# Count units placed inside the tiles of O and the neighbour projections, and every fourth unit's source one-hots made by VectorE

## The reference

```
xn = layernorm(x)
x  = x + sage_2_layers(xn, src, dst) + linear_attention(xn)      # Wq Wk Wv Wo
x  = x + moe(layernorm(x))                                       # 8 experts, top 2, and a shared expert
sage layer: h @ W_self + (segment_sum(h[src], dst) / degree) @ W_neigh + b
attention:  q = softmax over 64 of xn Wq; k = softmax over the nodes; (q (k^T v)) Wo + bo
```

## Time and profile before

| what | value |
|---|---|
| median of three runs | 1117.62 us |
| the profiled execution's own time | 1117.01 us |
| its span, first to last instruction | 1115.2 us |
| TensorE busy over the span | 1095.0 us |
| stage of the change, from the first matmul of O(0,0) to the first of the next stage | 224.86 to 362.81 us |
| TensorE, VectorE, ScalarE busy in these 137.95 us | 128.59, 84.93, 110.62 us |
| TensorE busy in the 197 us after it (363 to 560) | 197.00 us |

### The profile page before, as it was taken

How to read it: one execution, slowest core, us unless ns; L and a number is a source line. 1 busy time by engine, 2 the same in 40 slices (tenths; PEclk the granted TensorE clock), 3 DMA queues, 4 the chain that set the end, 5 groups by cost and what they waited for, 6 DMA issues and landing times.

```text
span 1115.2 us, 16441 instructions
## 1 busy us (share of the span) xinstructions
PE 1095.0 (98%) x6225; PEld 948.3 (85%) x6225; DVE 638.7 (57%) x880; ACT 482.3 (43%) x712; POOL 66.0 (6%) x88
## 2 busy tenths in 40 slices
PE   7999999999999999999999999999999999999998
PEld 5889998877777999878789999888988988988876
DVE  6789955765566744343373522445646556556545
ACT  4503321477888312211234222235655646556550
POOL 2000000000000000000000430200000000000003
PEclk9999999999999999999999999999999999999999
DMA  7222211232322022722004442377486676666647
GB/s 249 76 76 77 76 39 38 76 104 76 104 76 76 1 76 76 261 76 76 1 1 169 153 110 76 118 265 273 170 291 224 218 262 225 237 226 220 237 168 280
DMA packets 76488, 157.01 MB, mean 141 GB/s; under 512 B 7160, under 2 KB 7432, under 8 KB 76432
## 3 DMA queue, kind: packets, MB, share of 16 engines
q1 hardware_dynamic: 64908, 127.30, 33.3%
q10 hardware_dynamic: 7300, 15.41, 3.8%
q0 software_dynamic: 4224, 13.55, 3.7%
HBM read 135.69 MB, written 20.54 MB: 140 GB/s over the span
## 4 chain that ended last, share of the span: by engine, by line
PE 86%; DVE 4%; DVEq 3%; DMA 2%; issue 2%; ACT 1%; POOL 1%; POOLq 0%; SPq 0%; ACTq 0%
PE ps L1643 21%; PE ps L1645 20%; PE ps L1644 20%; PE ps L2055 10%; PE ps L2056 5%; DVEq L1356 2%; PE ps L1682 1%; PE ps L1728 1%; PE ps L1958 1%; PE ps L1959 1%; PE ps L1889 1%; PE ps L1890 1%; DVE c_f L1348 1%; DVEq L1349 1%; DMA y_second<-expert_rows,slots 1%
## 5 line engine op out<-in xcount | busy, mean ns | idle before, releaser
L991 DVE TENSOR_TENSOR w_lo<-w_raw,w_hi 128x2048 fp32r<-128x2048 f32 x108 | 244.7, 2290 | 136.8 <-ACT w_hi L685 134.7
L685 ACT CAST w_hi<-w_raw 128x2048 fp32r<-128x2048 f32 x108 | 203.5, 1911 | 87.8 <-PE ps L1959 36.2
L2055 PE MATMUL ps<-xe,w_hi 128*128 128x448 f32 x512 | 160.9, 375 | 0.0
L2056 PE MATMUL ps<-xe,w_lo 128*128 128x224 f32 x512 | 134.8, 263 | 0.0
L2055 PEld LDWEIGHTS ps<-xe,w_hi 128*128 128x128 f32 x512 | 95.9, 187 | 7.9
L1643 PE MATMUL ps<-w_hi,xt_hi 128*128 128x512 f32 (+1 forms) x240 | 96.0, 400 | 5.5 <-DVEq L999 4.3
L1643 PE MATMUL ps<-w_hi,he_hi 128*128 128x512 f32 (+1 forms) x256 | 101.2, 395 | 0.0
L1645 PE MATMUL ps<-w_hi,he_lo 128*128 128x512 f32 (+1 forms) x256 | 100.2, 391 | 0.0
L1644 PE MATMUL ps<-w_lo,he_hi 128*128 128x512 f32 (+1 forms) x256 | 100.0, 391 | 0.0
L2056 PEld LDWEIGHTS ps<-xe,w_lo 128*128 128x128 f32 x512 | 97.5, 190 | 0.4
L1645 PE MATMUL ps<-w_hi,xt_lo 128*128 128x512 f32 (+1 forms) x240 | 93.7, 390 | 0.0
(11 more groups left out here) (324 smaller groups left out, 1984.1 us busy)
## 6 DMA issues: line engine op xcount, KB each, us to landing
w_raw<-in_L_ffn_w SPq DMA_DIRECT2D x64, 1024.0 KB
w_raw<-in_L_gnn_W_neigh SPq DMA_DIRECT2D x8, 1024.0 KB
w_raw<-in_L_gnn_W_self SPq DMA_DIRECT2D x8, 1024.0 KB
w_raw<-in_L_ffn_shared_gate_up SPq DMA_DIRECT2D x8, 1024.0 KB
w_raw<-in_L_mix_Wv SPq DMA_DIRECT2D x4, 1024.0 KB
w_raw<-in_L_mix_Wk SPq DMA_DIRECT2D x4, 1024.0 KB
w_raw<-in_L_mix_Wq SPq DMA_DIRECT2D x4, 1024.0 KB
w_raw<-in_L_mix_Wo SPq DMA_DIRECT2D x4, 1024.0 KB
```

What stands on the lines that cost most here:

```text
L685: copy(w_hi[b][:, s * HK:(s + 1) * HK, :], w_raw[s][:, :, :]).then_inc(hi_done, 1)
L991: V_.tensor_tensor(w_lo[b][:, k, :], w_raw[s][:, :, :], as32(w_hi[b][:, k, :]), ALU.subtract).then_inc(lo_done, 1)
L2055: mat(PS(key)[:, a, 0:2 * B], wh[:, k, w_cols], xe[:, :, k, 0:B], start=k == 0, stop=False)
L2056: last = mat(PS(key)[:, a, 0:B], wl[:, k, w_cols], xe_hi[:, k, 0:B], start=False, stop=k == KF - 1)
```

## The change

Three things are changed.

1. **Place of the units on TensorE.** The units of a tile are issued inside the tile, after its k-steps 2, 4 and 6 (counted from 0; `AFTER_K`), and no longer behind its last matmul. So 9 matmuls of the tile stand ahead of the first unit, 6 between two units and 3 behind a third.
2. **Order on VectorE and ScalarE.** Both now deal with the tile's units first (additions and one-hots), then take the tile itself out of PSUM, then make the quarter of weights.
3. **Source one-hots.** For u = 3, 7, 11, ... 47 (12 units) VectorE makes the source one-hots in one comparison of 128x512, in an order with the two chunks of a pair interleaved; TensorE then reads that unit's weights with a stride of two elements. A copy `src16` of the list is made once for it.

The hand-out changes by one unit: units 0 to 2 now belong to O(0,0), unit 3 to O(0,1). The numbers of units in the five tiles of the halves are O(0,.) 3, 1, 2, 3, 3 (before: 2, 2, 2, 3, 3), O(1,.) 3, 1, 2, 3, 3, G(0,.) 3, 2, 1, 3, 3 and G(1,.) 3, 2, 2, 3, 3.

```diff
-    weights_to = [sum(2 if key[2] in SPLIT_AT else 3.5 for key in mains[:m + 1]) for m in range(len(mains))]
+    weights_to = [sum(1.625 if key[2] in SPLIT_AT else 3 for key in mains[:m + 1]) for m in range(len(mains))]
...
+    AFTER_K = (2, 4, 6)
+    by_vector = lambda u: u % 4 == 3
+    of_scalar = lambda u: sum(not by_vector(g) for g in range(u + 1))
...
             def source_one_hots(g):
                 b = g % GBUF
+                if by_vector(g):
+                    return
...
             for key in mains:                                   # ScalarE
+                for u in counts_in[key]:
+                    if u + GBUF < CU and not by_vector(u + GBUF):
+                        wait_unit(("cnt", u))
+                        source_one_hots(u + GBUF)
                 (attention_store if key[0] == "o" else neighbour_hi)(*key[1:])
                 if key[2] in SPLIT_AT:
                     split_hi(next_job(key), quarters=(SPLIT_AT[key[2]],))
-                for u in counts_behind[key]:
-                    if u + GBUF < CU:
-                        wait_unit(("cnt", u))
-                        source_one_hots(u + GBUF)
...
+                V_.tensor_copy(src16[:, :], list_s[:, :])
...
+                if by_vector(g):
+                    pairs_128 = [128, PER, 128, IL]
+                    V_.tensor_tensor(src_pairs(b), iota_c[:, 0:128, :].unsqueeze(1).to_broadcast(pairs_128),
+                                     src16[:, of_group].rearrange("p (q c) -> p q c", c=IL).unsqueeze(2).to_broadcast(pairs_128),
+                                     ALU.is_equal)
...
             for key in mains:                                   # VectorE
-                bins_at = load_bins(counts_behind[key])
-                (attention_out if key[0] == "o" else neighbour_lo)(*key[1:])
-                for n, u in enumerate(counts_behind[key]):
+                bins_at = load_bins(counts_in[key])
+                for n, u in enumerate(counts_in[key]):
                     add_counts(u, bins_at[PER * n:PER * n + PER])
                     if u + GBUF < CU:
                         one_hots(u + GBUF)
+                (attention_out if key[0] == "o" else neighbour_lo)(*key[1:])
                 if key[2] in SPLIT_AT:
                     split_lo(next_job(key), quarters=(SPLIT_AT[key[2]],))
...
                     last = passes(out_ap, [t[:, k, tokens] for t in operand], (wh[:, k, :], wl[:, k, :]),
                                   start and k == 0, stop and k == KF - 1)
+                    for after, u in zip(AFTER_K, inside):
+                        if k == after:
+                            count(u)
...
-            for key in mixed:
-                if key[0] == "cnt":
-                    count(key[1])
-                elif key[0] == "o":
+            for key in mains:
+                if key[0] == "o":
```

More of the change, by code:

```diff
@@ L124, in gps_layer @@
     units += mixed
-    counts_behind = {key: [k[1] for k in mixed[n + 1:mixed.index(mains[m + 1]) if m + 1 < len(mains) else None]]
+    counts_in = {key: [k[1] for k in mixed[n + 1:mixed.index(mains[m + 1]) if m + 1 < len(mains) else None]]
                      for m, key in enumerate(mains) for n in [mixed.index(key)]}
+    assert max(len(us) for us in counts_in.values()) < RING
+    AFTER_K = (2, 4, 6)
+    by_vector = lambda u: u % 4 == 3
+    of_scalar = lambda u: sum(not by_vector(g) for g in range(u + 1))
     chunks_of = lambda u: range(u * PC, min((u + 1) * PC, NC))
@@ L320, in gps_layer @@
         dst16 = following("dst16", [128, LC], f16, 2)
+        src16 = following("src16", [128, LC], b16, 2)
         assert off[0] <= RC + RCS
@@ L417, in gps_layer @@
         by_half = lambda ap: ap.rearrange("p (c n) -> p c n", c=2)
+        src_pairs = lambda b: src_oh[b][:, :, :].rearrange("p g n -> p (g n)").rearrange("p (q n c) -> p q n c", q=PER, c=IL)
         def halved(t, k, p=128):
@@ L802, in source_one_hots @@
                                          bias=src_f[:, g * GC + c:g * GC + c + 1]).then_inc(src_abs, 1)
-                act.wait_ge(src_abs, (g + 1) * GC)
+                act.wait_ge(src_abs, of_scalar(g) * GC)
                 nc.scalar.activation(src_oh[b][:, :, :], src_oh[b][:, :, :], ACT.Relu, bias=1.0, scale=-1.0).then_inc(src_ready, 1)
@@ L1650, in weights, with by_tokens @@
                 return w_hi[job % 2], w_lo[job % 2]
-            def by_tokens(key, out_ap, operand, job, tokens, start=True, stop=True, arrives=None):
+            def by_tokens(key, out_ap, operand, job, tokens, start=True, stop=True, arrives=None, inside=()):
                 wh, wl = w_hi[job % 2], w_lo[job % 2]
@@ L1738, in count @@
                 pe.wait_ge(oh_ready, u + 1)
-                pe.wait_ge(src_ready, u + 1)
+                if not by_vector(u):
+                    pe.wait_ge(src_ready, of_scalar(u))
                 for a in range(PER):
                     for c in range(CG):
-                        last = mat(PS(key)[:, a, 0:TD], src_oh[b][:, a * CG + c, :], dst_oh[b][:, a * TD:(a + 1) * TD, c],
+                        last = mat(PS(key)[:, a, 0:TD], src_pairs(b)[:, a, :, c] if by_vector(u) else src_oh[b][:, a * CG + c, :], dst_oh[b][:, a * TD:(a + 1) * TD, c],
                                    start=c == 0, stop=c == CG - 1)
@@ L1837, in attention_out @@
                 claim(key)
-                by_tokens(key, PS(key)[0:R(i), 0, :], AT, J_O + h, tile(i)).then_inc(ready[slot(key)], 1)
+                by_tokens(key, PS(key)[0:R(i), 0, :], AT, J_O + h, tile(i), inside=counts_in[key]).then_inc(ready[slot(key)], 1)
             def neighbours(h, i):
@@ L1845, in neighbours @@
                 claim(key)
-                by_tokens(key, PS(key)[0:R(i), 0, :], XT, J_L0 + h, tile(i)).then_inc(ready[slot(key)], 1)
-            for key in mixed:
-                if key[0] == "cnt":
-                    count(key[1])
-                elif key[0] == "o":
+                by_tokens(key, PS(key)[0:R(i), 0, :], XT, J_L0 + h, tile(i), inside=counts_in[key]).then_inc(ready[slot(key)], 1)
+            for key in mains:
+                if key[0] == "o":
                     attention_out(*key[1:])
```

## The result

| | before | changed |
|---|---|---|
| median of six runs | 1117.23 us | 1169.31 us |
| lowest and highest | 1115.69 to 1123.22 us | 1165.94 to 1180.62 us |
| ratio of the two, 95% interval | | 1.0469 (1.0439 to 1.0498) |
| stage of the change | 224.86 to 362.81 us | 225.15 to 416.85 us |

The kernel is 52 us slower; 1155 us had been forecast, with a range up to 1165. The stage has become 191.7 us long instead of 138, 54 us more. The profiled execution is the slowest of the six (1180.62 us): 10 of its 64 us come from the last stage, where in this one execution TensorE waited for `w_lo`, behind casts that waited for transfers of expert weights (54.4 us of such waits on ScalarE from 600 us on, 16.4 before).

The account below looks back on a forecast made before the run. TensorE, busy 1095.0 of 1115.2 us, was taken as the bound. Stage work 130.1 plus waits 44.0 gave 174.1 us, 36.1 more; 1117.0 + 36.1 = 1153.1, plus 2.1 for the clock, 1155 us; range 1140 to 1165.

Parts of the forecast that it names:

- The replay of the queues: Tile-by-tile count of TensorE's waits for VectorE and ScalarE in the changed stage: 44.0 us together.
- O(0,1): Its start waits 7.3 us, to 240.1, for VectorE's biases, register loads, three units and evacuation of the first tile.
- O(0,4), O(1,4): Each waits 5.4 us: VectorE, held by the second weight quarter, adds three units before emptying the buffer.
- G(0,4), G(1,4): Each waits 3.6 us: VectorE finishes w_lo 4.9 us into the tile before, then adds three units.
- TensorE's own time: Matmul work in the stage with units inside tiles: 130.1 us, 4.0 more than before.
- The side of "faster": Rival: evacuation fits beside the tile, 11.8 us of stage waiting goes, 4.0 of insertions come: 1109 us; chance of faster 0.06.
- the point named: Faster only if the mean wait behind the 12 tiles with three units is below 0.65 us.
- the clock's term: Slow matmuls after idling in the stage: one of three waits beyond 5 us costs 2.1 us.
- every long wait is paid for: Rival: five stage gaps of 3.6 to 7.3 us each cost 2.1 us: 1164 us; chance, or more, 0.15.
- the cast is hidden: Rival: VectorE's delay behind tiles 1 and 2 misses TensorE, 11.4 us less waiting: 1144 us; chance 0.17, including similarly smaller waits.
- The third part: VectorE's source one-hots for 12 units in the stage: 0.4 us each, 4.8 us counted in its cycles.

Follow-up runs that it names:

- experiment 7: Changed kernel with earlier hand-out, ScalarE's cast ahead of the one-hots, units after k-steps 0, 2 and 4, register loads without bounds checks: 1137.02 us, repeated 1134.82.
- experiment 1: Changed kernel with 14 to 40 matmuls on constants behind the last matmul of eight tiles, to fill TensorE's gaps: 1154.87 us.
- experiment 3: Changed kernel with ScalarE's cast of its w_hi quarter ahead of the tile's source one-hots instead of behind the tile's store: 1155.24 us.
- experiment 6: Kernel before with only the third part: VectorE makes every fourth unit's source one-hots, units stay behind the tiles: 1117.86 us against 1116.24.
- (5): Changed kernel without its third part, so ScalarE makes all source one-hots: 1164.31 us.
- (10): Kernel before without bounds checks of register loads, and VectorE making every fourth unit's source one-hots: 1111.59 us, beside 1111.37 without those one-hots.
- experiments 2 to 5: Four separate edits of the changed kernel: earlier hand-out 1163.97 us; cast ahead of one-hots 1155.24; units after k-steps 0, 2, 4 1161.42; ScalarE makes all source one-hots 1164.31.
- experiment 2: Changed kernel with the hand-out of the kernel before (2 units in O(0,0) and 2 in O(0,1)): 1163.97 us.

## Why the prediction was wrong

**Right: the work and the chain of waits.** The replay of the queues held to a fraction of a microsecond at nearly every place (in brackets, when O(0,1) starts):

| wait ahead of | forecast | measured |
|---|---|---|
| first units, in O(0,0) | 1.2 | 0.87 |
| O(0,1) | 7.3 (240.1) | 7.18 (240.40) |
| unit of O(0,3), O(1,3) | 1.2, 1.2 | 0.82, 1.20 |
| O(0,4), O(1,4) | 5.4, 5.4 | 6.04, 5.48 |
| O(1,0), O(1,1), G(0,0) | 1.7 each | 1.65, 1.54, 1.65 |
| G(0,1), G(1,1) | 2.8, 2.8 | 2.65, 2.65 |
| G(0,4), G(1,4) | 3.6, 3.6 | 3.76, 4.57 |
| G(1,0), next stage | 2.8, 1.6 | 2.75, 1.55 |
| all in the stage | 44.0 | 44.4 |

That the total is right to 0.4 us is in part luck: G(1,4) waited 1.0 us longer and O(0,4) 0.6, and most others a little less. The mechanisms are those forecast too. VectorE waited 2.40 us for the cast ahead of each of the four `w_lo` in the O tiles (13.5 us ahead of all eight), and in G(0,0) ScalarE came to `g_hi` behind two units' one-hots, at 332.43 us, 1.40 us ahead of the next tile's start (1.42 forecast). VectorE's comparison of 512 elements took 0.425 us (0.43 forecast, 12 of them). TensorE's own time was 131.3 us against 130.1. The side of "faster" fell on the point named: the mean wait behind the 12 tiles with three units is 3.5 us, far over 0.65, and even with the queues mended (experiment 7) it is 1.4 us behind 11 such tiles.

**Wrong: the clock's term, "I take one of the three, 2.1 us".** It measured 16 us by the sum over eight gaps, and 15.3 by experiment 1. Without it the sum was good to 1.6 us: 174.1 us of stage, against 191.7 - 16 = 175.7. Two things in the clock's term failed. The count: I let only gaps beyond 5 us be paid for, because the earlier trace rows show one of 5 us, and then took one of three. In the changed kernel's profile all gaps from 2.65 us on were paid for, and there were eight. The price, 2.1 us each, was right in the mean (16 / 8 = 2.0), which is in part luck: it came from one gap at the kernel's start, where the changed kernel's own execution shows 6.21 us for the same 19 matmuls and so 2.8, and single gaps cost 1.5 to 2.8. The rule of the Trainium skill that the prediction names, TensorE: Matmul & The Clock Gate, section "Why this matters for your kernels" (leave no idle gaps of a few microseconds between bursts of matmuls, or the clock goes back to half), was the better guide. The runs agree with it: each gap of 3.4 us and more was paid for, and some of 2.3 to 2.9 us too.

The rival "every long wait is paid for" came nearest with 1164. It took five gaps, and left out the three of 2.65 to 2.75 us. With eight at 2.1 the sum would have been 1153.1 + 16.8 = 1170. The rival "the cast is hidden" gave 11.4 us of waits for it; experiment 3, which hides it, measured 10.3 us (44.4 against 34.1), though the changed kernel itself does not hide it.

**The third part** was in the cycles with 4.8 us and nothing to set against it. It measures 2 us alone (experiment 6), 3 us of waits in the changed kernel (5), and nothing where VectorE has slack (10).

**Open.** Why the clock fell behind a gap of 2.34 us in one execution and not behind one of 2.33 in another is not settled. Nor are the 3 to 5 us between experiment 7's forecast and its times, beyond what one such fall explains, and how the loss divides between the units' place and the new order.

## What to carry to other kernels

Before work is moved out from between two tiles, ask what it covered there: count matmuls behind a tile gave VectorE time to empty the PSUM buffer that the next tile needs. Inside the tile they give none, and here they came with an order on the other engines in which that emptying is late. If a change makes TensorE idle for more than 3.4 us at a time, add some 2 us of half-rate work for each such gap to the sum. From 2.3 us on it can come, as here in every second case or so, and where it will come is not known. Leave it out only where TensorE would next wait for another engine anyway. And look at register loads in an engine's queue ahead of what others wait for: the bounds checks ahead of an evacuation were worth 5 us here.

## What the runs showed of the hardware

- The clock went down to its lower level (0.50 granted) in or behind each of the changed kernel's eight gaps of 2.65 us and more, and TensorE then worked at half pace for up to 6 us though it had no further waits; 1.5 to 2.8 us were lost each time. Behind its gaps of 1.54 to 1.65 us at most 0.15 us were lost, and the granted clock stayed at 1.00.
- In the five kernels with long gaps (changed, experiments 2 to 5) each of the 21 gaps of 3.42 us and more ahead of a tile cost 1.4 to 2.8 us. Between 2.2 and 3.1 us it went either way, and 13 of 24 such waits were paid for in all the profiles: 2.33 us cost nothing and 2.34 us cost 1.5 in two executions of the same kernel, in experiment 3 a gap of 2.79 us cost 0.1 and one of 2.38 us 1.7, and in experiment 2 one of 3.03 us cost nothing.
- Behind a shorter gap the clock can drop after the work has begun again: behind the 2.65 us ahead of 333.83 us the first five matmuls had their full pace, and the granted clock was 1.00 in the gap and 0.50 from 335.5 to 338 us.
- Matmuls on constants in the gap held the clock at 1.00 (40 in 6.81 us).
- A load of six values into VectorE's registers with their bounds checks took up to 2.73 us of its queue, and 3.09 us ahead of the changed kernel's first addition at 235.10 us.
